# Keys by tokens through the transposing DMA: 16-bit planes on GpSimd, the transpose in the DMA engines, interleaving on ScalarE

## The reference, cut to what matters

```python
Q = _phi((x @ Wq + bq).reshape(bs, n, H, D))      # _phi(x) = elu(x) + 1
K = _phi((x @ Wk + bk).reshape(bs, n, H, D))
V = (x @ Wv + bv).reshape(bs, n, H, D)
def step(carry, qkv):
    KV, Ks = carry
    KV = KV + jnp.einsum('bhd,bhe->bhde', ki, vi)
    Ks = Ks + ki
    num = jnp.einsum('bhd,bhde->bhe', qi, KV)
    den = jnp.einsum('bhd,bhd->bh', qi, Ks)
    return ((KV, Ks), num / (den[..., None] + EPS))
```

## Time and profile before

| | us |
|---|---|
| median of 3 runs | 1275.14 |
| lowest and highest | 1273.91, 1279.89 |
| the profiled execution's own time | 1273.15 |
| its span, from first to last instruction | 1271.4 |

### The profile page before, as it was taken

How to read it: one execution, slowest core, us unless ns; L and a number is a source line. 1 busy time by engine, 2 the same in 40 slices (tenths; PEclk the granted TensorE clock), 3 DMA queues, 4 the chain that set the end, 5 groups by cost and what they waited for, 6 DMA issues and landing times.

```text
span 1271.4 us, 48688 instructions
## 1 busy us (share of the span) xinstructions
PE 1244.6 (98%) x22173; PEld 1105.0 (87%) x22173; DVE 810.3 (64%) x2186; ACT 622.4 (49%) x1007; POOL 374.3 (29%) x590
## 2 busy tenths in 40 slices
PE   5899999999999999999999999999999999999997
PEld 5789888898988989889898988989889898898986
DVE  4675766757576574765757666575765758657473
ACT  4563654536446363653636445364553636536361
POOL 3424232132421413223142321324214132231320
PEclk9899999999999999999999999999999999999999
DMA  6000001000000000001000010000000000000000
GB/s 223 19 3 19 19 2 35 3 18 20 10 28 3 19 19 10 28 3 36 2 19 19 3 35 3 19 20 10 28 3 19 19 18 20 2 19 3 19 3 18
DMA packets 21597, 25.91 MB, mean 20 GB/s; under 512 B 1025, under 2 KB 19728, under 8 KB 21392
## 3 DMA queue, kind: packets, MB, share of 16 engines
q1 hardware_dynamic: 21392, 22.82, 5.5%
HBM read 14.43 MB, written 8.39 MB: 18 GB/s over the span
## 4 chain that ended last, share of the span: by engine, by line
PE 97%; DVE 1%; ACT 1%; DMA 1%; SPq 0%; issue 0%; DVEq 0%
PE s_pair L655 25%; PE w_pair L655 20%; PE o_pair L667 9%; PE s_pair L667 9%; PE o_pair L765 6%; PE kv_pair L740 5%; PE o_pair L779 5%; PE s_pair L729 5%; PE w_pair L709 4%; PE w_pair L702 4%; PE w_pair L689 3%; DMA ffn_tok<-in_L_ffn_Wout_w_dram 1%; DVE snaps L585 0%; SPq L267 0%; PE o_pair L655 0%; ACT ex L407 0%
## 5 line engine op out<-in xcount | busy, mean ns | idle before, releaser
L329 POOL TENSOR_SCALAR_AFFINE_SELECT aT<-aT 64x512 f32<-64x512 f32 x256 | 167.6, 655 | 833.0 <-ACT aT L434 824.7
L655 PE MATMUL w_pair<-xnT,wk 128*128 128x512 f32 x768 | 205.7, 403 | 0.7 <-ACT k_tok L420 0.7
L655 PE MATMUL s_pair<-xnT,wq 128*128 128x512 f32 x756 | 194.0, 392 | 0.0
L434 ACT ACTIVATE aT<-s_pair 128x512 f32<-128x512 f32 x128 | 76.4, 597 | 238.3 <-PE s_pair L729 238.3
L585 DVE TENSOR_TENSOR snaps<-kv_pair,snaps 128x65 f32<-128x65 f32 x768 | 173.3, 226 | 26.4
L520 DVE SCALAR_TENSOR_TENSOR kT<-w_pair,bias_one,ex 128x512 f32<-128x512 f32 x128 | 96.2, 751 | 122.7 <-ACT ex L410 122.6
L655 PEld LDWEIGHTS s_pair<-xnT,wq 128*128 128x128 f32 x756 | 142.1, 188 | 31.4
L655 PE MATMUL s_pair<-wv,xnT 128*128 128x512 f32 x648 | 168.7, 395 | 0.0
L410 ACT ACTIVATE ex<-ex 128x512 f32<-128x512 f32 x256 | 161.8, 632 | 8.1
L407 ACT ACTIVATE ex<-w_pair,neg_bias 128x512 f32<-128x512 f32 x130 | 89.5, 689 | 148.5 <-PE w_pair L655 148.5
L655 PEld LDWEIGHTS w_pair<-xnT,wk 128*128 128x128 f32 x768 | 136.1, 188 | 26.6 <-ACT k_tok L420 1.0
(11 more groups left out here) (105 smaller groups left out, 1953.7 us busy)
## 6 DMA issues: line engine op xcount, KB each, us to landing
x_in<-in_L_attn_x_dram SPq DMA_DIRECT2D x16, 512.0 KB, 3.9
out_dram<-y_buf SPq DMA_DIRECT2D x32, 256.0 KB, 2.1
stage<-in_L_attn_Wv_dram SPq DMA_DIRECT2D x2, 512.0 KB, 8.0
stage<-in_L_attn_Wk_dram SPq DMA_DIRECT2D x2, 512.0 KB, 9.6
stage<-in_L_attn_Wq_dram SPq DMA_DIRECT2D x2, 512.0 KB, 10.8
stage<-in_L_attn_Wo_dram SPq DMA_DIRECT2D x2, 512.0 KB, 9.1
bv_all<-in_L_attn_bv_dram SPq DMA_DIRECT2D x1, 512.0 KB, 8.6
ffn_tok<-in_L_ffn_Wq_dram SPq DMA_DIRECT2D x1, 256.0 KB
```

The costliest lines, as they stand in the source:

```text
L329: pool.affine_select(out=part, in_=part, compare_op=ALU.is_ge, fill=0.0, base=0, pattern=[[0, 2 * CH], [1, D]], channel_multiplier=-1).the ...
L434: act.activation(aT[:, n % 2].rearrange("p h c q -> p h (c q)"), s_pair[:, :, 0:CH * D], ACT.Copy).then_inc(s_copied, 1)
L655: last = pe.matmul(dst, l, r, start=i == 0, stop=i == len(steps) - 1)
```

## The change

The keys are made three units ahead instead of two; one more fill of keys, `("K", 2, 0)`, goes ahead of the loop. For unit 2 and all later ones `kT` is no longer transposed by PE. Instead:

1. POOL, `take_apart(m)`: when `phi` has made the keys of unit `m`, a copy of 1024 16-bit elements per partition splits the 32-bit words into a plane of low and a plane of high halves (`k_planes`). It stands in unit m-3 after `mask`, ahead of `residual`, `gates` and the levels.
2. SP, `turn_keys(m)`: one transposing DMA of 128 x 1024 16-bit elements (256 KB) from `k_planes` into `k_turned`, when the planes are there and `k_turned` has been read.
3. ACT, `put_together(m)`: a Copy of 1024 16-bit elements per partition interleaves the planes into `k_tok`. It stands in unit m-2 between `exponential` of the keys (of m+1) and `exponential` of the queries (of m). It waits for the DMA and until the outer products have read the previous `k_tok`.

`copy_keys` is left for units 0 and 1 only. PE waits for `k_whole` at the third transpose of `oT`. SP's stores of a block now come at the start of the next block, between the transposing DMAs.

```diff
@@ def unit_fills
-    ahead = divmod(n + 2, PAIRS) if n + 2 < blocks * PAIRS else None
+    keys = divmod(n + 3, PAIRS) if n + 3 < blocks * PAIRS else None
+    queries = divmod(n + 2, PAIRS) if n + 2 < blocks * PAIRS else None
...
-    if ahead:
-        fills += [(("K", ahead[1], ahead[0]), W0), (("Q", ahead[1], ahead[0]), S0)]
+    if keys:
+        fills.append((("K", keys[1], keys[0]), W0))
+    if queries:
+        fills.append((("Q", queries[1], queries[0]), S0))
     fills += [(name, S1) for name in tail]
+    fills.append((("oT", p, g), W1))
     if p == PAIRS - 1:
-        fills += [(("oT", p, g), W1), (("y", 0, g), O1)]
-    if ahead:
-        fills.append((("kT", ahead[1], ahead[0]), W0))
-    fills.append((("y", 1, g), S1) if p == PAIRS - 1 else (("oT", p, g), W1))
+        fills += [(("y", 0, g), O1), (("y", 1, g), S1)]
@@ SP
+            def turn_keys(m):
+                sp.wait_ge(k_apart, m - 1)
+                if m > 2:
+                    sp.wait_ge(k_whole, m - 2)
+                sp.dma_start_transpose(k_turned[:, :, :], k_planes[:, :, :].rearrange("p s t -> p (s t)"))\
+                  .then_inc(k_turned_in, 16)
...
+            turn_keys(2)
+            for n in range(UNITS):
+                g, p = divmod(n, PAIRS)
+                if p == 0 and g:
+                    store(g - 1)
+                if n + 3 < UNITS:
+                    turn_keys(n + 3)
@@ POOL
+            def take_apart(m):
+                g, p = divmod(m, PAIRS)
+                pool.wait_ge(drained[bank_of["K", p, g]], count_of["K", p, g])
+                if m > 2:
+                    pool.wait_ge(k_turned_in, 16 * (m - 2))
+                pool.tensor_copy(k_planes[:, :, :], kT[:, m % 2].bitcast(U16).rearrange("p (t s) -> p s t", s=2))\
+                    .then_inc(k_apart, 1)
+                pool.wait_ge(k_apart, m - 1)
...
                 if n + 1 < UNITS:
                     mask(n + 1)
+                if n + 3 < UNITS:
+                    take_apart(n + 3)
@@ ACT
+            def put_together(m):
+                act.wait_ge(k_turned_in, 16 * (m - 1))
+                act.wait_ge(kv_filled, m)
+                act.activation(k_tok[:, :, :].rearrange("p c f -> p (c f)").bitcast(U16)
+                               .rearrange("p (n s) -> p s n", s=2),
+                               k_turned[:, :, :].rearrange("p (s c) f -> p s (c f)", s=2), ACT.Copy).then_inc(k_whole, 1)
...
                     if kind in "KQ":
+                        if kind == "Q":
+                            put_together(n + 2)
                         exponential(name)
@@ PE
                         if c == 1 and g * PAIRS + i + 1 < UNITS:
                             until(a_masked, 2 * (g * PAIRS + i) + 4)
+                        if c == 2 and g * PAIRS + i + 2 < UNITS:
+                            until(k_whole, g * PAIRS + i + 1)
```

More of the change, by code:

```diff
@@ L9 @@
 F32R = mybir.dt.float32r
+U16 = mybir.dt.uint16
 P = 128
@@ L150, in attention_and_tree_layer @@
         k_tok = sb("k_tok", [P, CH, P])
+        k_planes = sb("k_planes", [P, 2, TOK], U16)
+        k_turned = sb("k_turned", [P, 2 * CH, P], U16)
         aT = sb("aT", [P, 2, 2, CH, D])
@@ L226, in attention_and_tree_layer @@
         kv_filled = sem("kv_filled")
+        k_apart = sem("k_apart")
+        k_turned_in = sem("k_turned_in")
+        k_whole = sem("k_whole")
         sum_ready = sem("sum_ready")
@@ L282, in _, with store @@
             load("wo1")
[L284 to L287, removed]
+            def turn_keys(m):
[4 more added lines that the diff above has]
+                  .then_inc(k_turned_in, 16)
+            def store(g):
                 for i in range(2):
@@ L292, in _ @@
                                  y_buf[:, 2 * i:2 * i + 2, :]).then_inc(y_stored, 16)
+            turn_keys(2)
[5 more added lines that the diff above has]
+                    turn_keys(n + 3)
+                if p == 2 and g + 2 < BLOCKS:
+                    sp.wait_ge(x_consumed, g + 1)
+                    sp.dma_start(x_in[:, g % 2], x_rows[g + 2]).then_inc(x_loaded[g % 2], 16)
+            store(BLOCKS - 1)
             sp.wait_ge(y_stored, 32 * BLOCKS)
@@ L419, in copy_keys @@
                 act.wait_ge(filled[bank_of[name]], count_of[name])
-                act.activation(k_tok[:, :, :].rearrange("p c n -> p (c n)"), psum_of(name), ACT.Copy)\
+                act.activation(k_tok[:, :, :].rearrange("p c f -> p (c f)"), psum_of(name), ACT.Copy)\
                    .then_inc(drained[bank_of[name]], 1)
+            def put_together(m):
[4 more added lines that the diff above has]
+                               k_turned[:, :, :].rearrange("p (s c) f -> p s (c f)", s=2), ACT.Copy).then_inc(k_whole, 1)
             def high_of_output(name):
@@ L468, in _ @@
             copy_keys(("kT", 1, 0))
+            exponential(("K", 2, 0))
             for n in range(UNITS):
@@ L515, in phi @@
             def phi(name):
-                kind, p, _ = name
-                slot, dst = (0, kT) if kind == "K" else (1, qT)
+                kind, p, b = name
+                slot, dst = (0, kT[:, p % 2]) if kind == "K" else (1, qT[:, p % 2])
                 col = p + (PAIRS if kind == "K" else 0)
                 dve.wait_ge(exp_ready, exp_count[name])
-                dve.scalar_tensor_tensor(out=dst[:, p % 2], in0=psum_of(name), scalar=bias_one[:, col:col + 1],
+                dve.scalar_tensor_tensor(out=dst, in0=psum_of(name), scalar=bias_one[:, col:col + 1],
                                          in1=ex[:, slot], op0=ALU.add, op1=ALU.max)\
@@ L615, in _ @@
             phi(("Q", 1, 0))
+            phi(("K", 2, 0))
             for n in range(UNITS):
@@ L701, in fill @@
                     for c in range(CH):
-                        last = pe.transpose(dst[:, c * P:(c + 1) * P], kT[:, i % 2, c * P:(c + 1) * P], ident[:, :])
+                        last = pe.transpose(dst[:, c * P:(c + 1) * P], kT[:, i, c * P:(c + 1) * P], ident[:, :])
                 elif kind == "oT":
@@ L785, in outer_products_when_ready @@
                 g, p = divmod(n, PAIRS)
-                until_drained(("kT", p, g))
+                if n < 2:
+                    until_drained(("kT", p, g))
+                else:
+                    until(k_whole, n - 1)
                 if p in (0, HALF):
@@ L876, in _ @@
             fill(("kT", 1, 0))
+            fill(("K", 2, 0))
             until(split_lo_pool, len(LO_POOL))
```

9 lines of the change are left out of this document (3 added, 6 removed).

## The result

| | before | after |
|---|---|---|
| median, us | 1275.43 (4 runs) | 1336.62 (4 runs, 1335.81 to 1338.0) |
| ratio, 95% interval | | 1.0476 (1.0452 to 1.0500) |
| span of the profiled execution, us | 1271.4 | 1336.3 |

A forecast was written before the change was run, and what follows sets the result against it. PE was taken as the bound (busy 98%, 97% of the chain); 1273.15 us profiled plus 20.5 for 16 blocks plus 3 at the start gave 1296.7, so 1297 us; range 1248 to 1365.

The forecast's parts named there:

- rival C: ScalarE's Copy: interleaved writes are slow, 2.42 us, making the relay 1.47 us later still; 1462 us, chance 5%.
- the forecast's own range: 1283 to 1315 us, from the Copy at 0.85 to 1.10 us and the start at 0 to 8 us.
- PE's new wait: PE's wait for k_whole at the third transpose of oT: costs nothing unless the DMA is late.
- the -0.44 of pair 7: Pair 7: the output projection stands between relay and scores, so the full 0.44 us of removed transposes is gained.
- The slack: Spare time between V's drain and the scores' start on PE, taken as 0.33 us a unit.
- 0.50 and 0.39 of loss from 0.83: Pairs 0, 1, 3, 4, 5: relay 0.83 us later, scores 0.50 later, or 0.39 in blocks that read state.
- relay: Keys' Relu and Exp, queries' Relu and Exp, queries' phi, V's drain, then PE's scores; forecast 0.83 us later.
- The start: The first detour has no full unit of PE work over it: 3 us, between 0 and 8.7.
- The closing sum: The profiled 1273.15 us plus 20.5 for the blocks plus 3 for the start: 1296.7 us.
- 1.84 and 1.09: Loss in us per block: 1.84 in a batch's first block (4 blocks), 1.09 in the other 12.
- A: ScalarE's Copy: 16-bit elements pass at half the time, holding ACT 0.48 us; 1252 us, chance 13%.
- B: Transposing DMA lands later than the 6.1 us allowed, so ACT waits; 1367 us at 8 us, 1680 at 10.8; 12%.

The follow-up runs named there:

- e3: The changed kernel with ScalarE's Copy moving the same bytes as 512 32-bit elements written flat, without interleaving and low halves: 1266.49 us.
- e4: The changed kernel with ScalarE's Copy behind the queries' Exp and without PE's early wait at oT: 1295.94 us.
- e5: The changed kernel with the interleaving copy on POOL in place of ScalarE and without PE's early wait at oT: 1226.46 us, 0.961 of the kernel before.
- e2: The changed kernel with ScalarE's Copy writing its 1024 16-bit elements flat, without interleaving and low halves: 1302.68 us.
- e1: The changed kernel without PE's wait for k_whole at the third transpose of oT: 1325.63 us, 1.0408 of the kernel before.
- e9: The changed kernel with the flat write of ScalarE's Copy and without PE's early wait at oT, both together: 1294.66 us.
- e7: The changed kernel without the detour (POOL's copy, transposing DMA, ScalarE's Copy and the waits for them) and without PE's early wait: 1221.06 us.
- e6: The changed kernel with ScalarE's Copy ahead of the keys' Relu and without PE's early wait at oT: 1328.75 us.

## Why the prediction was wrong in size

**The bound and the mechanism: right.** PE, bound at 98%; a Copy on ScalarE ahead of the queries' Relu; `phi` and V late in turn; PE waiting at the scores for V's drain in pairs 0, 1, 3, 4, 5 and for `qT` in 2 and 6; costless POOL copy and DMA. All are in the trace after, and e3, e4 and e5 change the time by shortening or moving that one Copy. One detail differs: in the five pairs PE first waits 0.4 us for `qT`, does the matmuls of S0, and then waits 0.3 for V, in place of one wait of some 0.9.

**The Copy on ScalarE: mis-sized, and the larger error.** "The nearest row is the split of a weight: 1.05 us" was a row of 32-bit elements written one behind the other. This one writes 16-bit elements 4 bytes apart and takes 1.36. I had held an upper bound for it only as rival C (2.42 us, 5%) and set the forecast's own range at 0.85 to 1.10. The 0.3 us stand in front of PE in all eight pairs: 34 us (e2), of the 40 by which the forecast missed. The Trainium skill's rate for ScalarE (ScalarE: Activation LUTs, "What ACT_TABLE_LOAD costs") gives 1.04 us for 1024 elements. The flat write agrees within 2 ns (1041), the interleaved one does not, by 0.31 us; the measurement decides.

**PE's new wait: wrong.** "PE comes there at 676.99 ... nothing, unless the DMA is late" was worked out for pair 1, where the fill of V lies between the queries and `oT`. Pair 7 has no V. PE comes to `oT` 1.4 us earlier against the Copy and stands 1.1 us. So the -0.44 of pair 7 became +0.83. Taking the wait out gives back 0.69 us of each pair 7, 11 us in all, at the Copy's real length (e1) as at the length that I had assumed (e9). The rest of pair 7 (19.98 against e7's 19.37) is `oT` itself coming late to the last tile of the projection, which I had not looked at, since I took all of pair 7 as cover.

**The slack: near, but read off the wrong row.** I had 0.33 us in a batch's first block and 0.44 in the others (0.50 and 0.39 of loss from 0.83). Both kinds of block behave alike and have 0.41 (0.65 lost of a relay 1.06 later; e7 has the same 0.41). The difference that I read off the scores' first row was one of matmuls of bank S0, not of those that wait for V.

**The start:** I had +3 us. Before the loop nothing was lost (it begins at 43.9 us, 45.8 before, which is within what two executions differ by), and block 0 grew by 3.6 us, less than the others. No run shows the 3 us. At the other end the last 20 us took 2.4 longer than before, with the clock at 0.50 for some 4 us of them; e1's execution has the same tail without it, so that is no part of the change.

**The closing sum:** with the Copy at 1.04 us and no early wait (e9) the kernel takes 1294.7 us and a block grows by 78.5 - 77.0 = 1.4 us; the prediction had 1.84 and 1.09, on average 1.3, and 1296.7. That this fits so closely is in part luck. Pair 7 gave back 0.13 us a block and not 0.44, the five pairs with V last lost 1.9 in place of 2.1, the 3 us at the start weren't there, and e9 is a single run beside one of the kernel before that lay 4 us above the others.

**The rivals.** A (half the time) is refuted by e2. B (late DMA) did not occur: 3.2 us against 6.1 allowed. C had the right instruction and direction, but the excess is a quarter of what it supposed (1.36 us over 1.05, not 2.42). The faster side existed, but not by the mechanism that I gave it: e5 gets there by another engine.

## What to carry to other kernels

Price an instruction by a row with its own access pattern, element width and step included; if there is none, the bounds belong in the forecast's own range. Work out a new wait in every kind of unit, above all in the one with fewer fills, since a long cover may lie behind the wait instead of ahead of it. And when work is taken off the busiest engine, look for the slack of the relay behind it first: the copy, with its early wait, cost 110 us more on the engine in the relay than the copy without the wait did on the one beside it, though both took 1.36 us for it; 99 of these are the place alone (e1 against e5).

## What the runs showed of the hardware

- A copy of 1024 16-bit elements per partition took 1.04 us on ScalarE written flat, 1.17 read alternately from two planes 1024 bytes apart, 1.36 written 4 bytes apart. POOL took 1.04 for reading 4 bytes apart and writing flat (the planes), and the same 1.36 for writing 4 bytes apart (e5). 512 32-bit elements took 0.62.
- A transposing DMA of 128 x 1024 16-bit elements, SBUF to SBUF, landed 3.1 to 5.0 us after its issue, 3.2 in the median, and held SP's queue 1.23 us. In the runs that moved the Copy the median was longer: 3.5 us in e5, 3.6 in e6, 4.0 in e4; why is open. The store of the same 256 KB landed in 2.1. The Trainium skill (VectorE: DVE Perf Modes, "The three transpose paths") has 1309 ns for one 128 x 128 tile, which as eight in a row I had estimated at 10.5 us: the trace does not agree with that estimate. Its rule that transposing DMAs are as fast as regular ones (Advanced Engine Details and Errata, "X-Bar Transpose (TRN2)") is nearer, though the store was 1.1 us faster.
- An instruction of DVE that reads and writes SBUF was slower beside POOL's interleaving copy. The normalisation of x (four instructions a block) takes 406 ns each before and 581 in e5. The excess is in those that overlap the copy: 16 of the 64, with 1085 ns in the mean and 1534 at most; the 45 with nothing on POOL beside them take 400. (Two beside `mask` take 600 and 800, in the changed kernel too.) First the kernel before, then e5:

```profile
L506 DVE TENSOR_SCALAR xn<-x_in,mean_var,rstd 128x256 f32<-128x256 f32 x64 | 22.0, 406 | 1.7 <-POOL rstd L313 1.7
```

```profile
L551 DVE TENSOR_SCALAR xn<-x_in,mean_var,rstd 128x256 f32<-128x256 f32 x64 | 33.4, 581 | 1.7 <-POOL rstd L337 1.7
```

The normalisation's neighbours that read PSUM kept their times: `phi` of the keys takes 751 ns in the 53 cases beside the copy and 748 with nothing on POOL. Pair 0 is no longer than in e7.
